# Eight single reductions in place of four paired ones in the attention norms, with new issue orders on all queues

## The chip, the cores and the metric

The kernel runs on one core of a Trainium2 chip. The metric is the device time of one execution in microseconds (us); lower is better. The core has a matrix engine (TensorE, PE in the profile), three elementwise engines (VectorE or DVE, ScalarE or ACT, GpSimd or POOL) and a queue that issues the transfers (SyncE or SP). They run side by side and meet at semaphores.

## The reference, cut to what matters

For each of 16 sequences of 512 tokens by 128 features the reference computes a Mamba-like block with a residual, and then two transformer layers with a residual:

```python
x = x + _layernorm(_L0_attn_ref(_layernorm(x), ...))   # state-space scan, 256 channels x 16 states
x = x + _layernorm(_L0_ffn_ref(_layernorm(x), ...))    # two layers of the kind below
# one layer, 8 heads of 64, windows of 64 tokens:
qkv = shift_token(x) @ wqkv
q, k, v = split(qkv)                    # per head
q = l2norm(q) * qs ; k = l2norm(k) * ksc
q, k = rotary_xpos(q, k)
o = local_attention(q, k, v)
x = x + o @ wo
h = layernorm(shift_token(x)) ; a, g = split(h @ w1 + b1)
x = x + (a * gelu(g)) @ w2 + b2
```

`l2norm` divides every head's 64 numbers by the root of their sum of squares. The change is about that sum.

## The kernel before, in words

The work is cut by sequence. A sequence goes through five streams of instructions: E (entry: layer norm, input projection, convolution, step sizes), M (the state-space scan), A (first transformer layer, with three PSUM banks f_bank), B (second layer, three banks b_bank) and C (the last layer norm and residual). F and S are short: step sizes, and spills to memory. In the loop over k, every engine's program holds work of several sequences at once: C of sequence k-1, B of k, A of k+1, M of k+2, E and S of k+3 (the table `AHEAD`). For k from 0 to 13 A, B and M are all present; call one such turn a full interval.

In which order an engine issues the pieces of its streams is written out in the strings `ORDER`, one for each engine: "A2 B1" means two pieces of A, then one of B. Each `yield` in a stream ends a piece. Engines run their queue strictly in this order, so a piece that waits holds up all behind it.

The M stream has 32 steps for each sequence. Step s needs the decay (ACT, L593, into the PSUM bank da), the feed (POOL, L645, dbu), the scan (DVE, L617, hs) and the read-out (POOL, L662, gy). After step 31 come the gate (POOL), the output projection (PE), a layer norm, x1 (POOL, L673) and another layer norm, whose result is the next A's input.

In A and in B each of 8 tiles (q0 q1 k0 k1 q2 q3 k2 k3) is projected by PE into a bank (L693), squared by ACT into one of two halves of `sq` (L787), rotated by DVE in two multiplications (L885 into m, L889 in place in the bank) and an addition into kr (L899), which frees the bank. After every second tile DVE sums the squares of both halves in one reduction (L872, `sum_squares(g)`), POOL clips the sums (L946), ACT takes logarithm and exponential (L803, L808/L810), and POOL scales both tiles (L954, `normalise`). PE transposes them (L341) and ACT copies them out (L824). Then come the scores, the maxima (DVE, L916, "peak"), the exponentials (ACT, L850), the values and the sums' reciprocals (DVE, L922, L925). The copy L960 lays out v for the windows.

`sp_enter` loads the entry tile of sequence k+3 into one half of B's `sq`, so it waits for B's last sum. `dve_norm_shift` (L330) makes the small operand mr_enter, mr_ff, mr_x or mr_out of a layer norm, from two SBUF inputs. L1107 adds the final residual on POOL; L1114 loads that residual.

## Time and profile before

| | |
|---|---|
| median of 3 runs | 2482.0 us (2479.64 to 2485.52) |
| the profiled execution | time 2485.52 us, span 2483.7 us |
| PE busy | 1934.9 us, 78% |
| DVE busy | 1919.8 us, 77% |
| ACT busy | 1830.6 us, 74% |
| POOL busy | 1778.2 us, 72% |
| DVE sums of squares (L872) | 128 of 1207 ns, 154.5 us |

Busy is the time in which an engine worked on an instruction, over the whole span with its start and its end, in which the pipeline of sequences fills and drains. Four engines are about equally busy, so the table doesn't say which is the bound; the order of the waits does. The profiled execution's time is 1.8 us more than its span, and 3.5 us more than the median.

### The profile page before, as it was taken

How to read it: one execution, taken by the hardware profiler on the slowest of the kernel's cores; microseconds unless marked ns; L12 is line 12 of the kernel's file. 1: busy time of each engine (PE TensorE's matmuls, PEld its weight loads, DVE VectorE, ACT ScalarE, POOL GpSimd, SP SyncE). 2: the span in 40 equal slices, each digit the busy share in tenths (PEclk: the TensorE clock that was granted, in tenths of full speed). 3: DMA queues.
4: the chain of work that ended last, by engine and by line, in shares of the span. 5: the costliest groups of instructions: out<-in, count | busy, mean ns of one | idle time of the engine just before them, and what ended most of it. 6: DMA issues, size and time to landing. Idle time of an engine off the chain costs nothing.

```text
span 2483.7 us, 44331 instructions
## 1 busy us (share of the span) xinstructions
PE 1934.9 (78%) x15936; PEld 1113.3 (45%) x15936; DVE 1919.8 (77%) x3509; ACT 1830.6 (74%) x4051; POOL 1778.2 (72%) x1668
## 2 busy tenths in 40 slices
PE   2156788797878888797878879797888879787866
PEld 0013355353635445353635445363645445363634
DVE  3557797978879797988879797988879797977442
ACT  2255788787878878786878878797878878686634
POOL 1969595977959596977959596886959596883020
PEclk9767999999999999999999999999999999999978
DMA  4443423333434333434433333434433333330000
GB/s 163 123 120 98 112 74 104 98 96 103 103 111 104 100 89 95 102 90 115 104 107 95 107 86 91 106 91 116 112 106 95 106 88 91 102 90 9 6 5 9
DMA packets 116107, 231.27 MB, mean 93 GB/s; under 512 B 24880, under 2 KB 57648, under 8 KB 115632
## 3 DMA queue, kind: packets, MB, share of 16 engines
q1 hardware_dynamic: 115888, 228.44, 34.5%
q8 instruction: 126, 2.06, 0.4%
q14 instruction: 93, 0.76, 0.1%
HBM read 185.42 MB, written 42.99 MB: 92 GB/s over the span
## 4 chain that ended last, share of the span: by engine, by line
DVE 30%; PE 28%; ACT 19%; issue 12%; POOL 2%; DMA 1%; DVEq 0%; SPq 0%; POOLq 0%; ACTq 0%
DVE hs L617 9%; DVE m L885 5%; ACT late L850 3%; DVE kr L899 3%; ACT da L593 3%; DVE b_bank L889 3%; PE b_bank L341 3%; DVE f_bank L889 2%; PE b_bank L719 2%; PE f_bank L341 2%; DVE ss L872 2%; PE b_bank L764 2%; DVE mx L916 2%; PE f_bank L995 2%; PE f_bank L1001 2%
## 5 line engine op out<-in xcount | busy, mean ns | idle before, releaser
L617 DVE TENSOR_TENSOR_SCAN hs<-da,dbu 128x512 f32<-128x512 f32 x512 | 622.3, 1215 | 112.8 <-POOL dbu L645 85.4
L662 POOL TENSOR_TENSOR gy<-hs,bc 128x512 f32<-128x512 f32 x512 | 650.4, 1270 | 44.9 <-DVE hs L617 40.9
L645 POOL TENSOR_TENSOR dbu<-spread,bc 128x512 f32<-128x512 f32 x512 | 649.5, 1269 | 9.2 <-DMA spread<-steps 9.2
L593 ACT ACTIVATE da<-spread,rest 128x512 f32<-128x512 f32 x512 | 359.1, 701 | 163.3 <-DVE hs L617 143.9
L954 POOL TENSOR_TENSOR kr<-kr,rn 128x512 f32<-128x512 f32 x256 | 263.6, 1040 | 18.7 <-ACT rn L810 15.3
L693 PE MATMUL b_bank<-rest,h_t 128*128 128x512 f32 x384 | 225.1, 687 | 49.2 <-DVE kr L899 40.8
L693 PE MATMUL f_bank<-rest,h_t 128*128 128x512 f32 x384 | 217.4, 653 | 56.5 <-DVE kr L899 49.3
L570 PE MATMUL y_sum<-gy,rest 128*32 128x512 f32 x1024 | 144.2, 638 | 87.9 <-POOL gy L662 87.9
L341 PE MATMUL b_bank<-first,kr 128*128 128x128 f32 x768 | 131.7, 307 | 97.0 <-DVE kr L899 61.5
L341 PE MATMUL f_bank<-first,kr 128*128 128x128 f32 x768 | 125.1, 291 | 100.3 <-DVE kr L899 63.3
L1107 POOL TENSOR_TENSOR xs<-xs,v 128x512 f32<-128x512 f32 x16 | 18.9, 1184 | 229.6 <-ACT xs L336 229.6
L341 PEld LDWEIGHTS b_bank<-first,kr 128*128 128x128 f32 x768 | 92.1, 154 | 187.3 <-DVE kr L899 145.5
L416 POOL TENSOR_TENSOR k_t<-k_t,m 128x512 f32<-128x512 f32 x32 | 39.9, 1269 | 184.5 <-ACT m L493 184.5
L341 PEld LDWEIGHTS f_bank<-first,kr 128*128 128x128 f32 x768 | 87.2, 146 | 163.3 <-DVE kr L899 108.9
L850 ACT ACTIVATE late<-b_bank,mx 128x128 f32<-128x128 f32 x512 | 139.0, 389 | 25.8 <-DVE mx L916 25.8
L872 DVE TENSOR_REDUCE ss<-sq 128x16 f32<-128x1024 f32 x128 | 154.5, 1207 | 0.0
L850 ACT ACTIVATE sq<-f_bank,mx 128x128 f32<-128x128 f32 x512 | 144.0, 395 | 9.4 <-DVE mx L916 7.8
L693 PEld LDWEIGHTS f_bank<-rest,h_t 128*128 128x128 f32 x384 | 70.8, 205 | 142.5 <-DVE kr L899 77.6
L693 PEld LDWEIGHTS b_bank<-rest,h_t 128*128 128x128 f32 x384 | 71.8, 213 | 121.8 <-DVE kr L899 65.5
L89 ACT ACT_TABLE_LOAD x82 | 105.2, 1283 | 20.2 <-DVE mv_enter L314 7.1
L885 DVE TENSOR_TENSOR m<-f_bank,tab 128x512 f32<-128x512 f32 x128 | 87.2, 681 | 35.3 <-ACT sq L787 35.3
L341 PE MATMUL b_bank<-first,late 128*128 128x128 f32 x512 | 84.6, 289 | 27.3 <-ACT late L850 25.6
(172 smaller groups left out, 4942.1 us busy)
## 6 DMA issues: line engine op xcount, KB each, us to landing
spread<-steps SPq DMA_DIRECT2D x256, 512.0 KB, 4.7
bc<-bc_rows SPq DMA_DIRECT2D x32, 512.0 KB, 6.8
steps<-k_t SPq DMA_DIRECT2D x32, 512.0 KB, 2.7
gate<-gates SPq DMA_DIRECT2D x32, 512.0 KB, 5.6
gates<-kr SPq DMA_DIRECT2D x16, 512.0 KB, 2.7
gates<-late SPq DMA_DIRECT2D x16, 512.0 KB, 3.4
sq<-in_x SPq DMA_DIRECT2D x16, 256.0 KB, 4.8
x<-in_x SPq DMA_DIRECT2D x16, 256.0 KB, 4.8
```

Of the source, the lines that this page charges most:

```text
L341: op = e.transpose(bank[:, n * P:(n + 1) * P], src(n), ident[:, :])
L570: op = e.matmul(y_sum[32 * j:32 * j + 32, :], sel[:, w, :], gy[:, 2 * j + k, :], start=w == 0 and k == 0, stop=w == 1 and k == 1, skip_gro ...
L593: e.activation(da[:, :], spread[:, slot(b, s // 2), 0, :], ACT.Exp, scale=a_neg[:, s:s + 1]).then_inc(decayed.sem, 1)
L617: e.tensor_tensor_scan(hs[:, s % 2, :], da[:, :], dbu[:, s % 2, :], 0.0, ALU.mult, ALU.add).then_inc(scanned.sem, 1)
L645: e.tensor_tensor(dbu[:, s % 2, :], spread[:, slot(b, s // 2), 1, :], bc[:, s % 2, :], ALU.mult).then_inc(fed.sem, 1)
L662: e.tensor_tensor(gy[:, s % 8, :], hs[:, s % 2, :], bc[:, 2 + s % 2, :], ALU.mult).then_inc(read_out.sem, 1)
L693: e.matmul(bank[:, :], w.h_t[:, t * P:(t + 1) * P], wqkv[:, l, part * INNER:(part + 1) * INNER], start=True, stop=True).then_inc(w.project ...
L850: op = e.activation(w.pr[:, hd % 2, p, :], X[hd % 2][:, p * P:(p + 1) * P], ACT.Exp, bias=w.mx[:, hd, p:p + 1])
L872: e.tensor_reduce(w.ss[:, 2 * g:2 * g + 2, :], w.sq[:, :, :].rearrange("p n (h d) -> p n h d", h=HEADS), AX, ALU.add).then_inc(w.summed.se ...
L885: e.tensor_tensor(halves(w.m2[:, n % 2, :]), halves(bank[:, :])[:, :, ::-1, :], table[1], ALU.mult).then_inc(w.rotated.sem, 1)
L889: e.tensor_tensor(halves(bank[:, :]), halves(bank[:, :]), table[0], ALU.mult).then_inc(w.rotated.sem, 1)
L954: e.tensor_tensor(x, x, w.rn[:, n, :].unsqueeze(2).to_broadcast([P, HEADS, DH]), ALU.mult).then_inc(w.normed.sem, 1)
```

## The change

The four reductions of 128x1024 (two tiles) of a layer become eight of 128x512. The signal `summed` counts 8 instead of 4. A tile's sum now comes before its rotation, where the paired sum came between the second tile's rotation and its addition. ACT's square of tile n waits for the sum of tile n-2, not of the pair. The first rotation's own wait on the square is gone, since the sum in front of it on the same engine waits for it. The strings `ORDER` are new for all five queues; the pieces themselves are otherwise the same.

```diff
-                self.squared, self.summed = s("squared", 8), s("summed", 4)
+                self.squared, self.summed = s("squared", 8), s("summed", 8)
...
-                E.wait_ge(*wb.summed(b - 3, 3))
+                E.wait_ge(*wb.summed(b - 3, 7))
...
                 if n > 1:
-                    E.wait_ge(*w.summed(b, n // 2 - 1))
+                    E.wait_ge(*w.summed(b, n - 2))
                 e.activation(w.sq[:, n % 2, :], bank_of(take)[:, :], ACT.Square)...
...
-            def sum_squares(g):
-                E.wait_ge(*w.squared(b, 2 * g + 1))
-                e.tensor_reduce(w.ss[:, 2 * g:2 * g + 2, :], w.sq[:, :, :]...(two tiles), AX, ALU.add)
+            def sum_squares(n):
+                E.wait_ge(*w.squared(b, n))
+                e.tensor_reduce(w.ss[:, n, :], heads(w.sq[:, n % 2, :]), AX, ALU.add)
...
-                E.wait_ge(*w.squared(b, n))      # in rotate(n)
...
+            sum_squares(0)
+            yield
             for n in range(8):
                 yield from rotate(n)
-                if n % 2:
-                    sum_squares(n // 2)
+                add(n)
+                yield
+                if n < 7:
+                    sum_squares(n + 1)
                     yield
-                add(n)
-                yield
...
-                E.wait_ge(*w.summed(b, g))       # in clip(g), POOL
+                E.wait_ge(*w.summed(b, 2 * g + 1))
```

Written out as instructions, the DVE queue from the last layer norm to the first scan was, and becomes (r, R: the two multiplications, a: the addition, SS: a paired sum, s: a single one; the letter in front is the stream):

```
before: C.stat C.aggr A.r0 C.mr A.R0 B.r0 A.a0 A.r1 A.R1 A.SS0 B.R0 A.a1 B.a0 B.r1 A.r2 B.R1 B.SS0 B.a1 scan0
after:  C.stat C.aggr C.mr A.s0 A.r0 B.s0 A.R0 B.r0 A.a0 B.R0 A.s1 B.a0 B.s1 B.r1 A.r1 B.R1 A.R1 B.a1 B.s2 A.a1 scan0
```

Around scans 9 to 11:

```
before: scan9 B.peak0 B.peak1 A.r7 A.R7 A.SS3 | scan10 A.a7 B.recip0 B.share0 B.peak2 B.peak3 | scan11
after:  scan9 B.peak1 E.stat | scan10 A.s7 A.r7 A.R7 B.recip0 B.share0 B.peak2 B.peak3 A.a7 | scan11
```

Around scans 24 to 26:

```
before: scan24 E.mr A.recip6 A.share6 | scan25 A.recip7 A.share7 | scan26 B.stat B.aggr
after:  scan24 A.recip5 A.share5 E.mr | scan25 A.recip6 E.pad A.share6 B.stat A.recip7 A.share7 | scan26 B.aggr
```

The start of POOL's queue (c: clip, q/k: normalise, v: the copy L960):

```
before: C.residual A.c0 A.q0 A.q1 A.v0 feed0 B.c0 feed1 B.q0 | gy0 ...
after:  C.residual A.c0 B.c0 A.q0 B.q0 feed0 feed1 B.q1 A.q1 A.v0 | gy0 ...
before: gy5 B.q3 B.v2 feed7 B.v3 A.c2 | gy6 feed8 B.c3 A.q2 B.k2 B.k3 | gy7 feed9 | gy8 feed10 A.q3 A.v2 A.v3 | gy9 A.c3 feed11 A.k2 | gy10 A.k3 feed12 | gy11
after:  gy5 B.q2 B.q3 B.v2 A.c2 feed7 B.v3 | gy6 B.c3 feed8 B.k2 B.k3 A.q2 | gy7 feed9 | gy8 feed10 | gy9 A.q3 A.v2 A.v3 feed11 A.c3 | gy10 A.k2 A.k3 feed12 | gy11
```

The start of ACT's queue was h0 h1 of A, h0 of B, C.ln, h1 of B, square A.q0, C.exp, square B.q0, square A.q1, C.normalise, v0 of A, square B.q1, ln and exp of A's first pair. It becomes: C.exp ahead of square A.q0, C.normalise ahead of both squares of q1, and v0 of B too ahead of A's ln and exp. SP loads the entry tile after the group load g5 where it was g7, and stores and residual loads move by some places.

## Rows read from the trace of the kernel before

**Rows 1.** The page: busy time and share of each engine.
```profile
PE 1934.9 (78%) x15936; PEld 1113.3 (45%) x15936; DVE 1919.8 (77%) x3509; ACT 1830.6 (74%) x4051; POOL 1778.2 (72%) x1668
```

**Rows 2.** Busy time by stretch: PE, PEld, DVE, ACT, POOL, clock, DMA, GB/s.
```profile
1249.00:1279.00 30.00, 28.65 (x119) 15.31 (x118) 15.95 (x50) 24.48 (x46) 7.58 (x7) 1.00 0.32 110
1279.00:1325.00 46.00, 30.64 (x139) 13.57 (x137) 44.46 (x59) 31.31 (x66) 43.56 (x47) 0.93 0.39 96
```

**Rows 3.** Timeline of POOL: start us, us, instruction, idle before it.
```profile
1245.78 1.27 POOL L662 TENSOR_TENSOR gy<-hs,bc 128x512 f32<-128x512 f32 x1 [0.98 <-DVE hs L617]
...
1278.91 1.19 POOL L1107 TENSOR_TENSOR xs<-xs,v 128x512 f32<-128x512 f32 x1 [5.11 <-ACT xs L336]
1280.64 0.24 POOL L946 TENSOR_SCALAR ss<-ss 128x16 f32<-128x16 f32 x1 [0.55 <-DVE ss L872]
1281.55 2.04 POOL L954 TENSOR_TENSOR kr<-kr,rn 128x512 f32<-128x512 f32 x2 [0.67 <-ACT rn L810]
...
1314.06 0.24 POOL L946 TENSOR_SCALAR ss<-ss 128x16 f32<-128x16 f32 x1 [1.01 <-DVE ss L872]
...
1316.98 0.24 POOL L946 TENSOR_SCALAR ss<-ss 128x16 f32<-128x16 f32 x1 [0.21 <-DVE ss L872]
...
1320.19 1.28 POOL L662 TENSOR_TENSOR gy<-hs,bc 128x512 f32<-128x512 f32 x1
...
1332.14 1.03 POOL L954 TENSOR_TENSOR kr<-kr,rn 128x512 f32<-128x512 f32 x1
```

**Rows 4.** Timeline of DVE in the rotation stretch.
```profile
1275.22 0.69 DVE L885 TENSOR_TENSOR m<-f_bank,tab 128x512 f32<-128x512 f32 x1 [1.66 <-ACT sq L787]
...
1282.26 0.68 DVE L885 TENSOR_TENSOR m<-b_bank,tab 128x512 f32<-128x512 f32 x1
1282.86 0.68 DVE L885 TENSOR_TENSOR m<-f_bank,tab 128x512 f32<-128x512 f32 x1
...
1312.77 1.21 DVE L872 TENSOR_REDUCE ss<-sq 128x16 f32<-128x1024 f32 x1
1313.89 0.68 DVE L885 TENSOR_TENSOR m<-b_bank,tab 128x512 f32<-128x512 f32 x1
...
1328.62 0.67 DVE L899 TENSOR_TENSOR kr<-f_bank,m 128x512 f32<-128x512 f32 x1
...
1329.92 1.29 DVE L916 TENSOR_REDUCE mx<-b_bank 128x4 f32<-128x512 f32 x2
```

**Rows 5.** Timeline of ACT at the start of an interval.
```profile
1274.59 0.60 ACT L787 ACTIVATE sq<-f_bank 128x512 f32<-128x512 f32 x1
...
1277.19 1.64 ACT L336 ACTIVATE xs<-xs,mr_out,rs_out 128x128 f32<-128x128 f32 x4
```

**Rows 6.** Timeline: the small operand mr_enter, and what POOL does meanwhile.
```profile
1226.43 3.04 DVE L330 SCALAR_TENSOR_TENSOR mr_enter<-mv_enter,rs_enter 128x4 f32<-128x4 f32 x1
...
1228.19 1.27 POOL L645 TENSOR_TENSOR dbu<-spread,bc 128x512 f32<-128x512 f32 x1
...
1231.23 1.28 POOL L662 TENSOR_TENSOR gy<-hs,bc 128x512 f32<-128x512 f32 x1 [1.78 <-DVE hs L617]
...
1788.89 0.14 DVE L330 SCALAR_TENSOR_TENSOR mr_enter<-mv_enter,rs_enter 128x4 f32<-128x4 f32 x1
```

**Rows 7.** Timeline of SP: the residual's load, once in an interval.
```profile
1083.31 2.62 SPq L1114 DMA_DIRECT2D v<-x_rows  x4
...
1224.24 2.72 SPq L1114 DMA_DIRECT2D v<-x_rows  x4
...
1786.34 2.56 SPq L1114 DMA_DIRECT2D v<-x_rows  x4
...
1926.41 2.56 SPq L1114 DMA_DIRECT2D v<-x_rows  x4
```

**Rows 8.** The waits of POOL: total us, times, longest.
```profile
POOL ss L946 <- DVE ss L872: 58.1, 53, 6.6
```

**Rows 9.** Timeline of DVE at the end, layer B alone.
```profile
2410.48 1.21 DVE L872 TENSOR_REDUCE ss<-sq 128x16 f32<-128x1024 f32 x1
```

More of the change, by code:

```diff
@@ L44 @@
     "pe": (
[3 rows of a table removed]
[3 rows of a table added]
     "act": (
[4 rows of a table removed]
[4 rows of a table added]
     "dve": (
[4 rows of a table removed]
[4 rows of a table added]
     "pool": (
-        "F4 C1 A4 M1 B1 M1 B1 M2 B1 M1 B1 M2 B1 M1 B3 M1 A1 M1 A2 M1 B1 M1 A1 B1 M1 B2 M1 B1 A1 M2 B1 A1 B2 M4 A3 "
-        "M1 A1 M1 A1 M1 A1 M44"),
-    "sp": "M1 F2 M10 E1 M2 C1 M6 B1 M2 S1 M1 S2",
+        "F4 C1 A1 B1 A1 B1 M2 B1 A2 M1 B1 M1 B1 M2 B2 M2 A1 B1 M2 B1 A2 M2 A1 M1 B3 A1 M1 B1 M1 B1 M1 B2 A1 M5 A3 "
+        "M1 A1 M1 A2 M44"),
+    "sp": "M1 F2 M6 C1 M2 E1 M12 B1 S2 M1 S1",
 }
@@ L867, in dve_attention @@
             bank_of = lambda take: w.banks[(TAKES.index(take) + 1) % 3]
-            def sum_squares(g):
-                E.wait_ge(*w.squared(b, 2 * g + 1))
-                e.tensor_reduce(w.ss[:, 2 * g:2 * g + 2, :], w.sq[:, :, :].rearrange("p n (h d) -> p n h d", h=HEADS), AX,
-                                ALU.add).then_inc(w.summed.sem, 1)
+            def sum_squares(n):
+                E.wait_ge(*w.squared(b, n))
+                e.tensor_reduce(w.ss[:, n, :], heads(w.sq[:, n % 2, :]), AX, ALU.add).then_inc(w.summed.sem, 1)
             def rotate(n):
```

22 rows, old and new, of the table ORDER are left out of this document.

## The prediction, made before the changed kernel was run

> **What bounds the kernel now.** The page comes first: four engines are within six points of each other [rows 1], so no total says which is the bound. A full interval is measured by a thing that happens once in it, the load of the residual: 1224.24 - 1083.31 = 140.93 us [rows 7]. There are 14 full intervals, some 1970 of the 2484 us.
>
> The busy time by stretch cuts the interval in three. In the tail (1249 to 1279) PE is busy for 28.65 of 30 us and POOL for 7.58. In the rotation stretch (1279 to 1325) DVE has 44.46 of 46 us and POOL 43.56, while PE and ACT have a third free [rows 2]. Behind it POOL works through feeds and read-outs. POOL's timeline shows how these hang together: in the rotation stretch it is idle only four times, 0.55, 0.67, 1.01 and 0.21 us, three of them for a sum of squares and one for the exponential behind it [rows 3]. So from 1280.6 on POOL's queue is the path, DVE is just ahead of it or just behind, and the tail is a chain through PE. A microsecond is worth one only where it takes an idle gap out of POOL or shortens the tail.
>
> **The split of the sums.** A single 128x512 sum from SBUF is not in the trace. Below, it can't cost less than half of the paired step: the paired sum starts at 1312.77 and the next instruction at 1313.89, 1.12 to 1.13 us, so 0.56. Above, it is a maximum of 128x512 without overlap, 0.69 (two take 1.29 us) [rows 4]. DVE instructions of this size otherwise follow each other in 0.60 us (1282.26 to 1282.86), and I take that. A pair then costs 2 x 0.60 - 1.13 = +0.07 us; eight pairs in an interval +0.56 us, with bounds of 0 and 8 x 0.25 = +2.0 us. It hides nowhere of itself, since DVE is full there; what counts is when POOL gets what it waits for.
>
> **What the earlier sums give.** I add up DVE's queue in both orders with 0.60 us for an instruction of this size and 1.13 for a scan or a paired sum. From A's first rotation to the end of A's third paired sum it is 37.6 us; the trace has 1313.98 - 1275.22 = 38.76, so 1.15 us of small waits [rows 4]. In the new order, from A.s0 to the end of A.s5, it is 36.2 us (the +0.07 included): the sum comes before two multiplications of its tile, not behind them. A.s0 starts some 0.2 us later than 1275.22, since C.exp (0.2 us) now stands ahead of A's first square at 1274.59 [rows 5] and the sum takes the place of the rotation. With 0.5 to 1.15 us of small waits A.s5 ends at 1312.1 to 1312.8, against 1313.98. But POOL's new queue also puts this clip earlier: from A.c2 to gy7 there were 5.9 us of work (1.23 a feed or read-out, 1.0 a scaling, 0.58 a copy, 0.2 a clip), now 7.7. So gy7 starts at 1319.8 to 1320.5, where it started at 1320.19 [rows 3]. I take -0.2 us. The same sum for B.c3 (4.4 us ahead of gy7, B.s7 ending near 1315) comes out at about the same time, so the two fit.
>
> **The start.** C.normalise moves ahead of both squares of q1, so the residual on POOL starts 0.8 us earlier than 1278.91; but A's logarithm now stands behind v0 of B as well. From the first squares on: normalise 1.64, two squares 1.1, four copies 2.2, which puts A.q0 at 1281.8 to 1282.1 in place of 1281.55 [rows 3, 5]. B's first scaling, however, follows at once and not 6 us later. That delay is smaller than the idle at A.c2, which is set by DVE; I cost it at nothing. If that gap is gone already, it costs 0.3 us.
>
> **Behind gy7.** A's last addition before was at 1328.62 to 1329.29, and POOL needed it at 1332.14: 2.8 us of slack [rows 3, 4]. In the new order it stands behind B.peak2 and B.peak3. Those end at 1331.21 in the trace, so the addition can't end before 1331.8. Slack of 0.3 us is left, and B's peaks themselves come 0.3 to 1 us later, because B.peak0 now stands before scan 9 and a square of A before the copies that free B's scores. Queued behind A.k3 on POOL is feed12, then all further scans. I take +0.2 us, bounds 0 and +1.2.
>
> **The small operand.** mr_enter takes 3.04 us at 1226.43 and 0.14 us at 1788.89; it is a 128x4 instruction. It ends at 1229.47, just as a POOL instruction does (1228.19 + 1.27), and the next read-out on POOL has waited for 1.78 us [rows 6]. With the long one an interval is 140.93 us, with the short one 1926.41 - 1786.34 = 140.07 [rows 7]: 0.86 us. I found it long in 8 of 13 intervals. In the new order it stands directly before scan 25, behind recip5 and share5. When it is long, the scan follows 0.5 us sooner, but five more pieces between scans 25 and 26 (2.0 us) then hold up gy26 by some 0.6: +0.1. When it is short, up to 0.5 us that these pieces cost before scan 25 is saved. Mean 0.6 x 0.1 - 0.4 x 0.5, about -0.15 us.
>
> The Trainium skill has a rule for this ("SBUF — State Buffer", "Who interferes with whom"): a DVE instruction with two SBUF inputs and a GpSimd instruction that reads SBUF take turns, and the later one blocks until the other is finished. The trace agrees in the end of the stall, but 3.04 us is more than one POOL instruction. By the page's rule a wait would be at most the rest of one POOL instruction, 1.27 us; with no long one left the sum would be 8 x 0.86 = 7 us lower, 2469 us, which is a part of the third rival below.
>
> **The tail.** PE's work behind the gate is the same in number and size. Moved there are B's first gating on DVE (now in an idle gap), parts of the projections, and SP's stores; the PE queue from the output projection to A's first transpose is full (rows 2: 28.65 of 30), and I find in the new order no piece whose input would come later than its turn. Zero, bounds -0.3 and +0.3 us. SP: the entry load stands behind g5 and waits for B.s7, which falls between scans 6 and 7; g6 behind it waits for scan 7 anyway, so no group is late. The residual load, behind x1's, has 20 us to spare.
>
> **The ends.** POOL waited for sums for 58.1 us in all [rows 8]; 14 intervals with 1.77 us make 25, so 33 us lie at the two ends, where one or two layers run without a full scan. There the chain is latency: square, sum, clip, logarithm, exponential, scaling. In the last layer the fourth paired sum ran from 2410.48 to 2411.69 [rows 9]; a single one would stand 1.3 us (two multiplications) ahead of 2410.48 and be done near 2409.8, 1.9 us earlier. The k3 scaling then waits for its addition, and 1.8 us are left. I count 1.8 for the last layer and about 1 each for the two other places: -4 us, bounds 0 and -8.
>
> **Sum.** A full interval: -0.2 + 0 + 0.2 - 0.15 + 0 = -0.15 us, times 14 = -2. With the ends -6 us. The profiled execution is 2485.5 us and would be 2479.5; it is 3.5 above the median, so for the median 2482.0 - 6 = 2476 us.
>
> **The rivals.** First, slower: A.k3 waits. Its price is the bound above, up to 1.2 us, plus the 0.3 of the start; with 0.9 us an interval, +12.6 - 4 = +9, so 2491 us, at the worst 2500. It decides from 0.6 us in an interval on. For it speaks that B's scores must now pass more of A; against it that 0.3 us of slack is there by the rows. Second, no change, 2482 us: DVE is as far behind as before at A.c2, since the split is added and ACT's logarithm sits behind copies, so that the earlier sum isn't used; the ends give 2 or 3 us and the split takes them. That is the case in which the change doesn't do what it says. Third, clearly faster: all waits of POOL for sums go (1.2 us) and mr_enter is short in every interval (0.86 in 8): 14 x 1.2 + 7 + 4 = 28 us at most, and with two thirds of it 2463 us. For it speaks that DVE's sums are 1.4 us earlier; against it that POOL asks 1.8 us earlier.
>
> **The numbers.** Forecast 0.38, slower rival 0.28, no change 0.22, clearly faster 0.12. This kernel's runs spread by some 0.2%, 5 us, and less than that can't be told from no change. The forecast lies at -6, so I put 0.31 of its 0.38 beyond the 0.2% and 0.07 within. Faster 0.31 + 0.12 = 0.43, same 0.22 + 0.07 = 0.29, slower 0.28. The range reaches from beyond the middle of the fast rival, 2455, to the bound of the slow one, 2500.
>
> **What would show it.** In the changed profile: 256 sums of 0.67 to 0.69 us with 0.60 between starts; POOL's waits for sums under 58 us by more than a half; gy7 45 to 46 us behind A's first square of the interval (1320.19 - 1274.59 = 45.6 now); a wait of POOL at A.k3 for an addition, under 0.5 us; the residual's load every 140 to 140.8 us. The prediction is wrong if that interval is above 141.2 or below 139.6 us, if mr_enter's mean leaves 1 to 2.5 us, or if PE is idle in the tail for more than 2 us.

## The result, and the profile after

The changed kernel takes 2496.53 us (median of ten runs, 2486.97 to 2500.3); the kernel before 2481.26 us beside it (2479.64 to 2486.24). The ratio is 1.0051 with a 95% interval of 1.0037 to 1.0065: slower by 0.5%, where the forecast was 2476 us and faster. The range of 2455 to 2500 us held it. The profiled execution has 2496.32 us and a span of 2494.5 us, against 2485.52 and 2483.7.

The page and the groups of DVE's instructions, for [rows 1] (busy us and share; in the groups: busy us, mean ns of one):

```profile
PE 1953.3 (78%) x15936; PEld 1124.2 (45%) x15936; DVE 1932.6 (77%) x3637; ACT 1825.5 (73%) x4051; POOL 1780.1 (71%) x1668
```
```profile
L871 DVE TENSOR_REDUCE ss<-sq 128x8 f32<-128x512 f32 x256 | 172.5, 674 | 34.6 <-ACT sq L787 34.3
```

The 256 single sums take 674 ns each. Busy time doesn't say where the 10.8 us of the span went: DVE has 12.8 us more, with 18.0 more in the sums (172.5 against 154.5 us) and 5 less elsewhere, and PE has 18.4 more for the same 15936 instructions, at a mean granted clock of 0.927 where it was 0.940. The order of the waits has to tell.

POOL's waits, for [rows 8] (total us, times, longest), and SP's residual loads, for [rows 7]:

```profile
POOL ss L945 <- DVE ss L871: 72.5, 63, 4.5
...
POOL kr L953 <- DVE kr L896: 7.5, 18, 1.9
```
```profile
811.60 2.51 SPq L1113 DMA_DIRECT2D v<-x_rows  x4
953.51 2.51 SPq L1113 DMA_DIRECT2D v<-x_rows  x4
...
1239.00 2.73 SPq L1113 DMA_DIRECT2D v<-x_rows  x4
1381.57 2.51 SPq L1113 DMA_DIRECT2D v<-x_rows  x4
...
1946.99 2.51 SPq L1113 DMA_DIRECT2D v<-x_rows  x4
2087.03 2.52 SPq L1113 DMA_DIRECT2D v<-x_rows  x4
```

Three lengths of interval: 141.91, 142.57 and 140.04 us, where [rows 7] has 140.93 and 140.07. To see where they differ I measure from the start of the last read-out (gy31) of the interval before to the start of each read-out on POOL. Each row is one interval; the others like it agree within 0.05 us. "Short" is an mr_enter of 0.57 us before and 0.33 us after:

| us behind the last gy31 | residual | gy0 | gy3 | gy7 | gy11 | gy14 | gy24 | gy31 |
|---|---|---|---|---|---|---|---|---|
| before, mr_enter short | 33.13 | 42.00 | 53.70 | 74.00 | 88.19 | 95.56 | 122.11 | 139.67 |
| before, mr_enter 3.02 us | 33.13 | 42.01 | 53.70 | 74.00 | 88.18 | 95.56 | 122.11 | 140.93 |
| after, mr_enter short | 32.28 | 43.31 | 54.22 | 74.11 | 88.62 | 96.27 | 122.63 | 140.04 |
| after, mr_enter 2.79 us | 32.29 | 43.31 | 54.21 | 74.11 | 88.62 | 96.28 | 122.65 | 141.78 |

Short against short the new kernel loses 0.37 us, long against long 0.85. Over the whole span (from the third row on mr_enter is made in another way, see e5 and e6 below):

| us | to the third sequence's gy31 | 12 intervals | next interval | the rest | span |
|---|---|---|---|---|---|
| before | 401.0 | 1686.6 | 138.7 | 257.4 | 2483.7 |
| after | 399.3 | 1702.4 | 139.2 | 253.6 | 2494.5 |
| before, other mr_enter (e5) | 397.4 | 1679.3 | 139.0 | 259.1 | 2474.8 |
| after, other mr_enter (e6) | 395.9 | 1685.0 | 139.2 | 253.8 | 2474.0 |

The ends gain about what was forecast (-1.7 and -3.8 us). The interval behind the twelve loses 0.5 us; the rest of the loss, 15.8 us, is in the twelve.

An undisturbed interval on POOL, from the residual on, the instructions that had to wait (for [rows 3]):

```profile
716.35 1.18 POOL L1106 TENSOR_TENSOR xs<-xs,v 128x512 f32<-128x512 f32 x1 [3.69 <-ACT xs L336]
...
718.97 0.24 POOL L945 TENSOR_SCALAR ss<-ss 128x16 f32<-128x16 f32 x1 [1.44 <-DVE ss L871]
...
720.15 0.24 POOL L945 TENSOR_SCALAR ss<-ss 128x16 f32<-128x16 f32 x1 [0.94 <-DVE ss L871]
...
750.51 0.24 POOL L945 TENSOR_SCALAR ss<-ss 128x16 f32<-128x16 f32 x1 [0.71 <-DVE ss L871]
```
```profile
770.45 1.04 POOL L953 TENSOR_TENSOR kr<-kr,rn 128x512 f32<-128x512 f32 x1 [0.28 <-DVE kr L896]
...
810.45 1.28 POOL L662 TENSOR_TENSOR gy<-hs,bc 128x512 f32<-128x512 f32 x1 [1.23 <-DVE hs L617]
...
813.63 1.27 POOL L662 TENSOR_TENSOR gy<-hs,bc 128x512 f32<-128x512 f32 x1 [0.67 <-DVE hs L617]
```

In the rotation stretch POOL waits 3.09 us for sums. Before, it waited 2.44 us in all in the interval of [rows 3]; that interval is itself 0.4 us late there (gy7 at 74.41), and an undisturbed one has 2.09 us in all, 1.42 of it for sums. So the waits moved to the start and grew. The 0.28 us at A.k3 are the wait that the slower rival named. The waits of 1.23 and 0.67 us are gy25 and gy26, behind mr_enter. The same place one stretch later, DVE above and POOL below:

```profile
1376.08 0.42 DVE L924 TENSOR_TENSOR kr<-f_bank,rd 128x256 f32<-128x256 f32 x1
1376.42 2.79 DVE L330 SCALAR_TENSOR_TENSOR mr_enter<-mv_enter,rs_enter 128x4 f32<-128x4 f32 x1
1379.14 1.21 DVE L617 TENSOR_TENSOR_SCAN hs<-da,dbu 128x512 f32<-128x512 f32 x1
...
1382.31 1.21 DVE L617 TENSOR_TENSOR_SCAN hs<-da,dbu 128x512 f32<-128x512 f32 x1
```
```profile
1376.68 1.28 POOL L662 TENSOR_TENSOR gy<-hs,bc 128x512 f32<-128x512 f32 x1
1377.90 1.29 POOL L645 TENSOR_TENSOR dbu<-spread,bc 128x512 f32<-128x512 f32 x1
1380.43 1.27 POOL L662 TENSOR_TENSOR gy<-hs,bc 128x512 f32<-128x512 f32 x1 [1.24 <-DVE hs L617]
```

mr_enter, the instruction that stalls, begins at 1376.42, while POOL works, and ends at 1379.21, 0.02 us behind POOL's last instruction (1377.90 + 1.29) before it has nothing to do. Then comes scan 25; scan 26 starts 3.17 us behind it instead of 2.5, since six pieces stand between (two stood there before). mr_enter is 2.76 to 2.80 us long in 9 of these 12 intervals; in the kernel before it is 3.02 to 3.04 us in 7 of the same 12. (The expectations below say 10 and 8: they count one more, ahead of the twelve.)

### The profile page after: what moved, and what is told of

The parts are those of the page before. It is cut to its first block and busy times, and to the rows that moved or that the text cites. A ratio compares the mean times of both kernels' runs of the same rounds, so it can differ in the third digit from the quotient of the medians.

```text
span 2494.5 us, 44349 instructions
## 1 busy us (share of the span) xinstructions
PE 1953.3 (78%) x15936; PEld 1124.2 (45%) x15936; DVE 1932.6 (77%) x3637; ACT 1825.5 (73%) x4051; POOL 1780.1 (71%) x1668
## 5 line engine op out<-in xcount | busy, mean ns | idle before, releaser
L693 PE MATMUL b_bank<-rest,h_t 128*128 128x512 f32 x384 | 237.2, 714 | 64.2 <-DVE kr L896 55.7
L341 PE MATMUL f_bank<-first,kr 128*128 128x128 f32 x768 | 136.2, 311 | 83.3 <-DVE kr L896 62.4
L871 DVE TENSOR_REDUCE ss<-sq 128x8 f32<-128x512 f32 x256 | 172.5, 674 | 34.6 <-ACT sq L787 34.3
L341 PE MATMUL b_bank<-first,kr 128*128 128x128 f32 x768 | 121.4, 294 | 98.1 <-DVE kr L896 86.3
L341 PEld LDWEIGHTS f_bank<-first,kr 128*128 128x128 f32 x768 | 94.8, 156 | 138.8 <-DVE kr L896 90.6
L737 PE MATMUL f_bank<-vs,m 128*64 128x65 f32 x1024 | 87.2, 229 | 33.3 <-DVE kr L924 21.3
```

What stands on the lines that cost most here:

```text
L341: op = e.transpose(bank[:, n * P:(n + 1) * P], src(n), ident[:, :])
L693: e.matmul(bank[:, :], w.h_t[:, t * P:(t + 1) * P], wqkv[:, l, part * INNER:(part + 1) * INNER], start=True, stop=True).then_inc(w.project ...
L737: op = e.matmul(ot[WIN * j:WIN * j + WIN, p, :], w.p_t[:, hd % 2, q0:q0 + WIN], (w.vs, w.v)[j][:, p, hd, :], start=True, stop=True)
L871: e.tensor_reduce(w.ss[:, n, :], heads(w.sq[:, n % 2, :]), AX, ALU.add).then_inc(w.summed.sem, 1)
```

## The experiments

All times are medians; the kernel before ran beside each on the same chip (2481.5 to 2483.0 us up to e12, 2488.91 for e13 to e16). No ratio to the kernel before reaches 2%, apart from e4's. A profile is a single execution: where it lies far from the median, the text says so. A ratio is of this to that, with its 95% interval.

**e1: scans 24 to 27 as before.** In the changed kernel, DVE's pieces from scan 23 to scan 28 stand in the order of the kernel before.

```diff
-scan23 A.peak6 A.peak7 | scan24 A.recip5 A.share5 E.mr | scan25 A.recip6 E.pad A.share6 B.stat A.recip7 A.share7 | scan26 B.aggr | ...
+scan23 A.peak6 A.peak7 A.recip5 A.share5 | scan24 E.mr A.recip6 A.share6 | scan25 A.recip7 A.share7 | scan26 B.stat B.aggr | ...
```

> The changed kernel with one stretch of DVE's queue as before: from scan 23 to scan 28 recip5 and share5 of A stand before scan 24, mr_enter directly behind scan 24, recip6 and share6 before scan 25, B's statistics behind scan 26. Everything else is the changed kernel. Theory T (the larger part of the loss comes from this stretch: A.share6 has gone behind scan 25, so PE's V7 and the entry's transposes behind it in PE's queue are late, ACT's copy of them holds up decay 27, and B's statistics hold up scan 26): the load of the residual comes every 140.9 to 141.3 us where mr_enter is long, in place of 141.8 to 143, and 2481 to 2487 us in all. Rival R1 (the loss sits in the rotation stretch, and what is late there shows again later): under 3 us better than the changed kernel, 2490 to 2494.

2518.63 us (1.0139, 1.0118 to 1.0159): much slower than either theory. mr_enter is short (0.14 us) in nearly every interval, and it doesn't help: DVE waits for PE's values before each reciprocal of A, 71.7 us (61 times) where the changed kernel waits 14.2 (29 times), and gy24 comes 1.05 us later. A's attention is later in the new queues, so the old place of recip5 is too early for it. This refutes mr_enter's place as something that can be put back alone, but says nothing yet of the stall itself.

**e2: the split alone,** in the queues of before, both sums at the place of the paired one.

```diff
-                e.tensor_reduce(w.ss[:, 2 * g:2 * g + 2, :], ..., AX, ALU.add).then_inc(w.summed.sem, 1)
+                for n in (2 * g, 2 * g + 1):
+                    e.tensor_reduce(w.ss[:, n, :], heads(w.sq[:, n % 2, :]), AX, ALU.add).then_inc(w.summed.sem, 1)
```

> The kernel before with all its queues, the paired sum cut into two single sums one behind the other at the same place. Theory T (DVE is full in the rotation stretch and POOL waits for its sums there, so each step more of DVE is paid): +0.07 us a pair, +0.56 us in a full interval, +8 us in all, 2489. Rival R2 (the added steps fall into DVE's small waits or behind work of POOL): within 2 us of the kernel before, 2480 to 2483.

2489.15 us (1.0025, 1.0011 to 1.0040): the time that theory T said. Its size is partly luck: intervals are 140.08 and 141.35 us, each 0.4 longer and not 0.56, the added time first shows at gy7 (74.4 to 74.9), and e11 below has 3.8 us for the split where no stall adds to it.

**e3: paired sums in the new queues.** The changed kernel, but an even tile's sum is left out and the odd one's covers both.

```diff
-                e.tensor_reduce(w.ss[:, n, :], heads(w.sq[:, n % 2, :]), AX, ALU.add)...
+                if n % 2:
+                    e.tensor_reduce(w.ss[:, n - 1:n + 1, :], ...(both halves), AX, ALU.add)...
```

> The changed kernel with all its new queues, but paired sums: the piece of an even tile's sum is empty, the piece of an odd tile's sum does the pair. Theory T (the loss is the queues' own, the split adds 0.56 us an interval on top): 5 to 8 us better than the changed kernel, 2486 to 2489, so still slower than before. Rival R2 (the split costs nothing that is paid): as the changed kernel, 2492 to 2496. Rival R3 (it is the split alone that makes it slower): as the kernel before, 2481.

2501.93 us (1.0072, 1.0049 to 1.0095), above all three expectations: these queues need single sums.

**e4: early single sums in the old queues.** Each sum directly ahead of its tile's first rotation, as in the changed code.

```diff
                 E.wait_ge(*w.squared(b, n))
+                e.tensor_reduce(w.ss[:, n, :], heads(w.sq[:, n % 2, :]), AX, ALU.add).then_inc(w.summed.sem, 1)
                 e.tensor_tensor(halves(w.m2...), ...)
```

> The kernel before with all its queues; every tile has a single sum directly before its first rotation, in the same piece, and the old piece of the paired sum is empty. Theory T (POOL's waits for sums in the rotation stretch, 1.2 us an interval, are what the earlier sum can give back, the split costs 0.56): -0.2 to -0.6 us in a full interval and about -4 us at the ends, 2470 to 2478. Rival R4 (POOL's queue asks for the norms at fixed places, so that an earlier sum gives nothing and only delays the bank's release): +0.5 us an interval, 2486 to 2490.

2532.9 us (1.0201, 1.0178 to 1.0223). Far above both theories. POOL now waits 24.0 us (10 times) for sums, but 62.0 us (63 times) for ACT's exponential behind them, and gy7 is 3.2 us late. An early sum on DVE gives nothing in these queues of ACT and POOL. The code and the queues of this change belong together.

**e5 and e6: mr_enter without its second SBUF input.** The same edit on the kernel before (e5) and on the changed one (e6):

```diff
-            e.scalar_tensor_tensor(mr[:, :], mv[:, :, 0], -1.0, rs[:, :], ALU.mult, ALU.mult)
+            for t in range(NT):
+                e.tensor_scalar(mr[:, t:t + 1], mv[:, t, 0:1], rs[:, t:t + 1], -1.0, ALU.mult, ALU.mult)
```

> The kernel before; only mr_enter (128x4 from two SBUF inputs, 3.04 us in 8 of its 13 intervals) is made in four DVE instructions of 128x1, each from one SBUF input and a scalar per partition, on the same place of the queue. Theory T (the form with two inputs stalls beside POOL, and an interval with the stall is 1.28 us longer: 140.95 against 139.67): no long mr_enter, all full intervals at 139.7 to 140.1 us, about 8 x 1.28 = 10 us less, 2471 us (2468 to 2475). Rival R5 (the stall stands for a wait on something else that the next DVE instruction would inherit, or the four small ones stall as well): intervals of 140.95 remain, 2479 to 2484 us.

> The changed kernel with the same edit of mr_enter. There a long one was found in 10 of 12 full intervals, and an interval with it was 1.74 us longer than one without (141.78 against 140.04). Theory T (about half of the loss against the kernel before comes from more and dearer stalls): about 10 x 1.74 = 17 us less than the changed kernel, 2479 us (2475 to 2484), and the gap between the changed kernel and the one before shrinks from 13 to 15 us to 5 to 9 with the stall out of both. Rival R6 (the stall only hides work that was late anyway): 2488 to 2496 us, and the gap stays at 13 or more.

e5: 2476.61 us (0.9975, 0.9964 to 0.9985), between the two theories: 6 us less where 10 were expected. e6: 2473.2 us (0.9959, 0.9947 to 0.9971), 23 us less than the changed kernel and less than the kernel before; that is below both theories, which had 5 us or more of loss left. So the stall was priced too high in the old queues and too low in the new ones. e6's group of DVE, and SP's residual loads of it:

```profile
L391 DVE TENSOR_SCALAR mr_enter<-mv_enter,rs_enter 128x1 f32<-128x1 f32 x64 | 9.1, 204 | 1.9 <-ACT rs_enter L325 1.9
```
```profile
1222.88 2.73 SPq L1116 DMA_DIRECT2D v<-x_rows  x4
1363.47 2.51 SPq L1116 DMA_DIRECT2D v<-x_rows  x4
1503.18 2.52 SPq L1116 DMA_DIRECT2D v<-x_rows  x4
```

mr_enter no longer stalls: none of the 64 instructions takes over 0.21 us. The intervals of these rows are 140.59 and 139.71 us. By the table of spans the stall costs 20.5 us in the changed kernel (2494.5 - 2474.0) and 8.9 in the kernel before (2483.7 - 2474.8). That difference of 11.6 is the whole loss of 10.8; the rest of the change gives 0.8 us in the span. Without the stall the twelve intervals are still 5.7 us longer than in e5, and the two ends 6.8 us shorter. By the medians the difference is larger, 23.3 against 6.0 us.

**e7: A's last addition first,** ahead of B.peak2 and B.peak3: the slower rival of the prediction.

```diff
-scan10 A.s7 A.r7 A.R7 B.recip0 B.share0 B.peak2 B.peak3 A.a7
+scan10 A.s7 A.r7 A.R7 B.recip0 B.share0 A.a7 B.peak2 B.peak3
```

> The changed kernel with A's last addition moved from behind B's third and fourth maxima to ahead of them, on DVE; nothing else. This is the step that the prediction's slower rival rests on: POOL waits at A.k3 for that addition. In the changed kernel's profile that wait is 7.5 us in all (18 times). Theory T (it is worth its 0.3 us in an interval and no more; the loss is elsewhere): 2490 to 2496 us, the waits for an addition on POOL gone, the stretch from gy7 to gy11 14.2 us in place of 14.5. Rival R7 (the late addition delays all that is queued behind A.k3 and is the main cause): 2480 to 2487 us.

2497.25 us (1.0054, 1.0042 to 1.0066), no change against the changed kernel, 1 us above theory T's range. POOL's waits for an addition fall from 7.5 to 2.4 us and gy11 is at 88.31 in place of 88.62, but gy14 at 96.36 in place of 96.28: what POOL gains it gives back three scans later. The rival's mechanism is there and isn't the cause.

**e8: B's first addition 1.2 us earlier,** to keep PE's first wait short.

```diff
-A.s0 A.r0 B.s0 A.R0 B.r0 A.a0 B.R0 A.s1 B.a0
+A.s0 A.r0 B.s0 A.R0 B.r0 B.R0 B.a0 A.a0 A.s1
```

> The changed kernel with B's first addition 1.2 us earlier on DVE: the queue before scan0 runs A.s0 A.r0 B.s0 A.R0 B.r0 B.R0 B.a0 A.a0 A.s1 in place of A.s0 A.r0 B.s0 A.R0 B.r0 A.a0 B.R0 A.s1 B.a0. In the changed kernel PE waits 1.99 us for that addition at the start of each interval, and in four or five intervals the granted clock falls right behind it, the next projections take 1.3 to 2.1 us for two in place of 1.0 to 1.1, and gy3 comes 0.3 to 0.9 us late; in the kernel before PE waits 1.70 us there and the clock falls later. Theory T (the shorter wait keeps the clock up through the projections): PE's wait 0.8 us, no interval with gy3 above 54.4 us behind the last read-out of the interval before, 4 to 5 us less than the changed kernel, 2491 us (2488 to 2494). Rival R8 (the clock falls whatever that wait is): gy3 late in as many intervals, 2495 to 2498 us.

2494.3 us (1.0037, 1.0023 to 1.0050), between the two theories; its profile is the slowest of the seven runs (2501.34). Two intervals of the changed kernel, and then one of e8, projections on PE (us, and the wait ahead of them):

```profile
719.53 1.13 PE L693 MATMUL b_bank<-rest,h_t 128*128 128x512 f32 x2 [1.99 <-DVE kr L896]
720.50 1.02 PE L693 MATMUL f_bank<-rest,h_t 128*128 128x512 f32 x2
...
1288.72 1.31 PE L693 MATMUL b_bank<-rest,h_t 128*128 128x512 f32 x2 [1.99 <-DVE kr L896]
1289.83 1.91 PE L693 MATMUL f_bank<-rest,h_t 128*128 128x512 f32 x2
1292.30 2.08 PE L693 MATMUL b_bank<-rest,h_t 128*128 128x512 f32 x2 [0.56 <-DVE kr L896]
```
```profile
722.68 1.13 PE L690 MATMUL b_bank<-rest,h_t 128*128 128x512 f32 x2 [1.06 <-DVE kr L893]
723.65 1.02 PE L690 MATMUL f_bank<-rest,h_t 128*128 128x512 f32 x2
727.45 1.89 PE L690 MATMUL b_bank<-rest,h_t 128*128 128x512 f32 x2 [2.79 <-DVE kr L893]
```

The same two stretches of the changed kernel by engine: length, busy us of PE, PEld, DVE, ACT and POOL, and then the granted clock (1.00 is 2.4 GHz, 0.50 would be 1.2 GHz all the time), DMA share and GB/s:

```profile
718.00:728.00 10.00, 5.95 (x12) 2.03 (x12) 10.00 (x17) 7.74 (x16) 8.09 (x10) 1.00 0.78 177
1287.00:1297.00 10.00, 7.73 (x10) 2.67 (x11) 9.35 (x16) 6.25 (x15) 7.91 (x10) 0.66 0.90 210
```

Behind the same wait of 1.99 us the next pairs of projections take 1.02 us in one interval and 1.91 to 2.08 in the other. In the late interval gy3 comes 0.3 us late and gy7 0.6. In e8 the first wait is shorter and the second grows to 2.79 us, and the clock falls behind it in 12 of 13 intervals. gy3 is at 54.6 or later in all of them, but 0.38 of that is there at gy0 already (43.69 against 43.31); from gy0 to gy3 it is 10.9 us in most of them, as in an undisturbed interval. So e8 does not test the price of the clock: the move shifted the gap and made gy0 late.

**e9: both gaps at once,** on e6: A.s1 behind B.a0, and A.R1 behind B.a1.

```diff
-A.a0 B.R0 A.s1 B.a0 B.s1 B.r1 A.r1 B.R1 A.R1 B.a1
+A.a0 B.R0 B.a0 A.s1 B.s1 B.r1 A.r1 B.R1 B.a1 A.R1
```

> The changed kernel with the stall out (2473.2 us, intervals of 140.07 us, but four of 140.5 to 141.4), and two pieces moved on DVE ahead of scan0: A.s1 from ahead of B.a0 to behind it, A.R1 from ahead of B.a1 to behind it, so that both of B's additions come 0.6 us earlier. PE waits for them at the start of each interval, 1.99 and 1.59 us; with only the first wait shortened (1.06) and the second longer (2.79) the clock fell in every interval. Theory T (the two idle gaps together bring the clock down, and that makes the long intervals): gaps of 1.4 and 1.6 us or less, the granted clock 1.00 from 34 to 44 us behind the last read-out in all or nearly all intervals, gy3 never above 54.4 us, about 3 us less, 2470 us (2467 to 2472). Rival R9: the clock falls in as many intervals as before, 2473 to 2476 us.

2477.5 us (0.9985, 0.9976 to 0.9993), 4 us more than e6 and above both theories. The gaps are 1.53 and 1.73 us, and no interval has gy3 above 54.51: the late starts are gone. The falls of the clock are not: between 34 and 44 us behind the last gy31 it falls in 5 of 13 intervals, as in e6, but always behind the second gap, where it doesn't delay gy3 (in e6 four of the five came behind the first). gy0 and all behind it are 0.27 us later in nearly every interval, 12 x 0.27 = 3 us. In the profile, the fastest of the eleven runs (2473.89), the two cancel: twelve intervals are 1684.6 us against e6's 1685.0. What makes the median 4 us longer is not shown.

**e10: one more instruction of that form,** in e5, with constants as inputs and a tile as output that nobody reads, directly behind scan 15.

```diff
+                if s == 15:
+                    e.scalar_tensor_tensor(spare[:, :], conv_w[:, 0, :], -1.0, conv_w[:, 1, :], ALU.mult, ALU.mult)
```

> The kernel before with the stall out (2476.6 us), and one more DVE instruction of the form of mr_enter (128x4, two SBUF inputs, here constants, into a tile that nobody reads) directly behind scan15 of each sequence, where POOL works through feeds and read-outs without a pause. It does nothing for the result. Theory T (the form itself stalls beside a busy POOL and holds the next scan): the added instruction takes 1 to 3 us in most sequences, intervals 1 to 2.5 us longer, 2490 to 2512 us. Rival R10 (mr_enter's 3 us came from its neighbours on the queue or from what it read, not from the form): 0.14 to 0.16 us each, 2475 to 2479 us.

2508.66 us (1.0106, 1.0092 to 1.0120), 32 us more than e5. The added instruction on DVE, and POOL beside it:

```profile
1350.95 3.14 DVE L624 SCALAR_TENSOR_TENSOR spare<-first 128x4 f32<-128x4 f32 x1
```
```profile
1352.77 1.30 POOL L651 TENSOR_TENSOR dbu<-spread,bc 128x512 f32<-128x512 f32 x1
1356.57 1.28 POOL L668 TENSOR_TENSOR gy<-hs,bc 128x512 f32<-128x512 f32 x1 [2.50 <-DVE hs L621]
```

It takes 3.05 us in the mean of 16, ends at 1354.09 as POOL runs out of work (1352.77 + 1.30 = 1354.07), and the next read-out waits for 2.50 us: the interval is 142.3 to 142.7 us in place of 139.7 to 140.2. So neither mr_enter's neighbours nor its data are needed for the stall; an instruction of its form beside a busy POOL is enough.

**e11 and e12: the two halves of the change, without the stall.** e11 is e2 and e12 is e3, each with the edit of e5.

> The kernel before with every paired sum cut in two on its place (the earlier run of that alone gave 2489.2 us, +6.1), and the stall out. Theory T (split +0.4 us an interval whatever the stall does): 2476.6 + 6 = 2482.5 us (2480 to 2485). With the changed kernel without the stall at 2473.2 us the new queues then give 9 us to single sums. Rival R11 (part of the 6 us was the stall, longer or more often): 2476 to 2480 us.

> The changed kernel's queues with paired sums (the earlier run of that gave 2501.9 us), and the stall out. Theory T (stalls of 1.74 us in some ten intervals made most of the loss against the kernel before, and singles are worth 5 us in these queues): 2501.9 - 20 = 2482 us (2477 to 2485). Rival R12 (the new queues themselves are slower, stall or not): 2488 to 2497 us.

e11: 2480.39 us (0.9995, 0.9987 to 1.0004), at the lower edge of theory T. e12: 2485.85 us (1.0021, 1.0010 to 1.0032), between the two theories. All eight medians (of chips on which the kernel before took 2481.3 to 2483.0 us):

| us | paired sums | single sums |
|---|---|---|
| old queues | 2481.3 to 2483.0 | 2489.2 (e2) |
| new queues | 2501.9 (e3) | 2496.5 (the change) |
| old queues, no stall | 2476.6 (e5) | 2480.4 (e11) |
| new queues, no stall | 2485.9 (e12) | 2473.2 (e6) |

Without the stall, the split alone costs 3.8 us and the new queues alone 9.2; together they give 3.4. The stall takes 5 to 9 us in the old queues and 16 to 23 in the new ones.

**e13: fewer pieces behind the stall.** In the changed kernel B.stat, A.recip7 and A.share7 go behind scan 26.

```diff
-scan25 A.recip6 E.pad A.share6 B.stat A.recip7 A.share7 | scan26 B.aggr
+scan25 A.recip6 E.pad A.share6 | scan26 B.stat A.recip7 A.share7 B.aggr
```

> The changed kernel, stall and all, with B.stat, A.recip7 and A.share7 moved from ahead of scan26 to behind it on DVE, so that behind the stalled mr_enter and scan25 three pieces (A.recip6, E.pad, A.share6) stand ahead of scan26 and not six. Theory T (a stall costs 1.74 us in the new queue and 1.28 in the old one because those six pieces are pushed into scan26's turn): intervals with a stall 141.3 us or less in place of 141.78, 4 to 6 us less, 2491 us (2488 to 2493). Rival R13 (scan26 is late for another reason, or the three pieces only push scan27): 2494 to 2500 us.

2529.09 us (1.0163, 1.0150 to 1.0176), far above both theories. DVE and ACT there:

```profile
676.66 0.42 DVE L921 TENSOR_TENSOR kr<-f_bank,rd 128x256 f32<-128x256 f32 x1
...
679.24 1.22 DVE L614 TENSOR_TENSOR_SCAN hs<-da,dbu 128x512 f32<-128x512 f32 x1 [1.86 <-POOL dbu L642]
```
```profile
677.83 0.60 ACT L860 ACTIVATE q_t<-f_bank 128x512 f32<-128x512 f32 x1 [2.09 <-PE f_bank L338]
678.46 0.69 ACT L590 ACTIVATE da<-spread,rest 128x512 f32<-128x512 f32 x1
```

share7 (676.66) is needed by PE's transposes, ACT's copy waits 2.09 us for these, and the next decay (678.46) stands behind the copy. So these three pieces can't go later without a cost. The price of a stall did fall from 1.74 to 1.37 us (144.18 against 142.81), as theory T has it, but the wait on ACT costs more.

**e14: mr_enter in front of recip5 and share5.**

```diff
-scan24 A.recip5 A.share5 E.mr | scan25
+scan24 E.mr A.recip5 A.share5 | scan25
```

> The changed kernel, stall and all, with mr_enter moved in front of A.recip5 and A.share5, directly behind scan24, as it stands in the kernel before. Theory T (what a stall costs is set by what DVE has left to do before the next scans, and that is the same work here): 2494 to 2500 us, intervals with a stall 141.6 to 142.1 us, as many of them. Rival R14 (the place half a microsecond later made it long more often): stalls in half of the intervals or fewer, 2484 to 2491 us.

2504.02 us, 2482.65 to 2510.61 in twelve runs (1.0048, 1.0029 to 1.0068). In its profile the stall has three lengths: 3.57 us four times, with intervals of 143.5 to 145.2 us; 1.12 to 1.15 us six times and 0.14 twice, with 140.1 to 141.2. A long one on DVE with POOL beside it, then one of the middle kind:

```profile
808.45 3.58 DVE L327 SCALAR_TENSOR_TENSOR mr_enter<-mv_enter,rs_enter 128x4 f32<-128x4 f32 x1
```
```profile
808.26 1.30 POOL L642 TENSOR_TENSOR dbu<-spread,bc 128x512 f32<-128x512 f32 x1
809.50 1.29 POOL L659 TENSOR_TENSOR gy<-hs,bc 128x512 f32<-128x512 f32 x1
810.72 1.29 POOL L642 TENSOR_TENSOR dbu<-spread,bc 128x512 f32<-128x512 f32 x1
```
```profile
952.24 1.15 DVE L327 SCALAR_TENSOR_TENSOR mr_enter<-mv_enter,rs_enter 128x4 f32<-128x4 f32 x1
```
```profile
952.09 1.27 POOL L642 TENSOR_TENSOR dbu<-spread,bc 128x512 f32<-128x512 f32 x1
953.32 1.27 POOL L659 TENSOR_TENSOR gy<-hs,bc 128x512 f32<-128x512 f32 x1
```

Both begin 0.15 to 0.19 us behind the start of a feed. One ends with that feed, the other three instructions later. The median is above both theories, though on this chip the kernel before is slower as well: by its ratio e14 stands where the changed kernel does (1.0051). In the profile theory T's count and price are wrong. At a place 0.7 us earlier long stalls are rarer, 4 of 12, as the rival had it, and dearer, 3.5 us of interval. But this execution, 2494.91 us, is 9 us under the median, so how many long ones a usual run has is not shown.

**e15 and e16: e5 and e6 side by side.**

> The kernel before with mr_enter made without the form that stalls, once more, on the same chip as the next one: 2476.6 us before, 2475 to 2479 us now by every theory.

> The changed kernel with the same edit, on the same chip. Theory T (without the stall the change does what was forecast, some 2 to 6 us): 2 to 6 us less than the run beside it, 2471 to 2475 us. Rival R16 (the earlier gap was chance; the gain at the ends is given back by the late starts of some intervals): within 1.5 us of the run beside it.

2476.22 and 2474.86 us (0.9952, 0.9939 to 0.9964, and 0.9944, 0.9932 to 0.9956); spans 2474.4 and 2474.2. The gap is 1.4 us here, within what the rival R16 allows, and was 3.4 above. Without the stall the change is thus 1 to 3 us faster, which is within the 0.2% that count as no change; the forecast gain of 6 us isn't there. The kernel before took 2488.91 us on this chip, 6 us more than on the others, and e5's twin didn't follow it.

## Why the prediction was wrong

The step that failed is "The small operand". It counted mr_enter at -0.15 us an interval, 0.6 x 0.1 for the long case and 0.4 x -0.5 for the short, with the same share of long ones before and after. From gy24, just ahead of mr_enter, to gy31 the table of intervals has:

| us from gy24 to gy31 | long | short | long ones in twelve |
|---|---|---|---|
| before | 18.82 | 17.56 | 7 |
| after | 19.13 | 17.41 | 9 |

So the long case costs 0.31 more and not 0.1, the short one saves 0.15 and not 0.5, and the long case is more frequent. In the mean of these twelve intervals that is +0.41 us where the step had -0.15. e5 and e6 confirm the direction and make it larger, by taking the stall away: -8.9 us in the span of the kernel before and -20.5 in the changed one, -6.0 and -23.3 in the medians. The step had -2 us for all of it. The mechanism in the long case was right. In the new queue gy25 does follow gy24 half a microsecond sooner (3.74 us against 4.27), and gy26 then follows 0.71 us later than it did, for a forecast 0.6. (The step spoke of five more pieces and 2.0 us; there are four more, about 1.5 us.) The stall's length was right too, and its price in the old queue too low, 0.86 for a measured 1.28 us, because [rows 7] compared a long interval with a disturbed short one.

The half microsecond gave nothing all the same, because gy24 itself is 0.52 us late. This is the second wrong size: earlier sums, start and "Behind gy7" added up to 0 in the sum. gy7 is 0.11 late, and another 0.41 comes behind it, where 0.2 were forecast; e7 rules out the wait at A.k3 as its cause, and no run isolates another.

The excess of an interval is 1702.4 - 1686.6 = 15.8 us in twelve, 1.32 each: 0.52 up to gy24 and 0.41 behind it. The remaining 0.4 are intervals longer than either usual length. Four start late (gy3 at 54.5 to 55.1), where the granted clock fell behind PE's first wait; some lose 0.3 to 0.6 us at scans 26 and 27, whose cause I did not find. The late starts vary from execution to execution: e6 has four intervals with gy3 at 54.5 or later, e16 three, in other places. Without the stall the twelve lose 5.7 us (e6 against e5). Of the other 10.1 us the counted stalls (9 x 1.74 against 7 x 1.28) are 6.7; the rest isn't assigned.

The prediction's third rival held the right mechanism (mr_enter short everywhere, worth 7 us) and gave it to the change; it took an edit that the change didn't contain. That the measured 2496.5 us lies inside the stated range is no credit to it: the range reached that far for the wait at A.k3, which e7 refutes.

Point by point:

- **Split, +0.07 a pair, 0.56 an interval.** Starts stand 0.60 us apart, 674 ns each. In place it cost 0.34 us an interval without the stall (e11 against e5, in twelve) and 0.4 with it (e2). Right in kind, at two thirds of its size.
- **Earlier sums, gy7 -0.2 us.** gy7 is at 74.11 against 74.00: in the range given, without the gain. The 45.6 us from A's first square to gy7 were read in the late interval of [rows 3]; an undisturbed one had 45.19 before, and it is 45.05 now, with the square 0.25 us later.
- **The start, nothing or 0.3.** The residual is 0.84 us earlier as said, but the first two clips wait 1.44 and 0.94 us, and gy0 is 1.3 us late, 1.0 of which is B.q1, which now stands ahead of it on POOL; gy3 is 0.5 late, gy7 0.1, except where the clock fell.
- **Behind gy7, +0.2.** The wait at A.k3 is 0.28 us, and gy11 is 0.43 late in place of 0.11. e7 shows that taking it away gives nothing: gy14 is then as late as before.
- **"POOL's waits for sums less than half of 58".** Wrong: 72.5 us. The earlier sums were used up by earlier clips, as the text feared for one place.
- **The tail, nothing.** Right: 28.66 of 30 us PE busy in the same stretch.
- **The ends, -4.** Right, within its bounds: -3.8 us at the end and -1.7 at the start; -5.3 and -1.5 between e5 and e6.
- **Rivals.** A.k3 (2491 us) lay nearest to the measured time for a reason that e7 refutes. No change (2482 us) is what is left without the stall.

Before the change, the profile could not have told how often mr_enter would be long in its new place. It could have told to look: the rows had it long in one interval and short in another with no wait in sight, and the half microsecond that the step set against its +0.6 could only be kept if gy24 came on time.

Open: what lets mr_enter through at some starts and not at others, and with it how often a given kernel stalls. The old kernel's spread over chips (2475.7 to 2491.3 us, while e5 and e15, on two chips, stay within 2475.7 to 2479.7) fits a varying number of stalls, but only single executions were profiled.

## What to carry to other kernels

- When a tiny instruction shows microseconds of busy time, price it by what is queued behind it in the new order, and better, take the form away first: four instructions of 128x1 with one SBUF input each were 6 us faster than one of 128x4 with two in the old queues and 23 us in the new ones. That turned a loss of 15 us into a gain of 1 to 3.
- Judge a new order only with such stalls out of both kernels. An experiment with two factors, with and without the stall, told in four runs what single moves (e1, e13, e14) blurred.
- The order of one engine's queue can't be judged alone: putting four scans' worth of DVE's pieces back (e1) or moving three of them behind one scan (e13) cost 22 and some 28 us more than the change, each through another engine's queue.

## What the runs showed of the hardware

A DVE instruction of 128x4 with two SBUF inputs, started while POOL runs feeds and read-outs back to back, takes until a POOL instruction ends (0.26 to 1.26 us), or until POOL has nothing left (2.34 to 3.76 us); only one that starts as a POOL instruction ends, or with POOL idle, takes 0.14 us. It ends 0.02 to 0.03 us behind a POOL instruction. The start alone doesn't decide: in the kernel before, begun 0.70 to 0.73 us into a feed, it took 3.02 to 3.04 us eight times and 0.57 us once. mr_ff, the same form between other neighbours, never waited for more than one POOL instruction (0.77 us at most in 576 executions of all profiles). Each POOL row of e14 begins 0.06 to 0.07 us before the one ahead has ended, which fits a long wait; that this is its cause is not shown.

The four 128x1 instructions, each with one SBUF input and a scalar for each partition, took 0.20 us each beside the same POOL. e5 changed the operation, the width and the number of SBUF inputs at once, so the runs don't separate these three. The Trainium skill ("SBUF — State Buffer", "Who interferes with whom") says that a DVE instruction with at most one SBUF input, outside its two-port modes, doesn't contend with GpSimd and that one with two does; e5, e6 and e10 agree. The same page of the Trainium skill ("Summary: rules for kernel authors") says that the one that issues second blocks until the first is finished. The waits of 0.26 to 1.26 us agree. The long ones differ: at 808.45 the instruction passed over two ends of a POOL instruction before it ran, and by that rule it would have cost at most 1.3 us.

The granted clock falls behind short waits of PE, and not each time: after 1.99 us of idle PE the next projections ran at 1.02 us a pair in one interval and at 1.91 in another. In the kernel before, with gaps of 1.70 and 1.27 us, the clock stayed at 1.00 from 34 to 44 us behind the last gy31 in all 13 intervals and fell later, behind a gap of 2.07 us or more at 44; in the changed one it fell there in 7 of 13, and gy3 was late in the four of them in which it fell behind the first gap.
